# Subtractions of a recurrence moved to TensorE, scaling moved to ScalarE, and a new order of pieces in one stage

## The reference

```
x = x + tanh(g_xattn[0]) * attention_over_heads(layernorm(x), ctx)     # stages A, B, G0
x = x + tanh(g_ffn[0])   * mixture_of_16_experts(layernorm(x))         # top 6 and a shared one: G0, H0
x = x + tanh(g_xattn[1]) * wkv(w, u, k=layernorm(x), v=ctx)            # stage M
x = x + tanh(g_ffn[1])   * mixture_of_64_experts(layernorm(x))         # top 8: routing in M, then H1, I1

def layernorm(x): return (x - mean) / sqrt(var + 1e-5)
def wkv step, per sequence and channel, over 64 positions (p, q, o are carried):
    no  = max(o, u + k);   A  = exp(o - no);      E  = exp(u + k - no)
    y   = (A * p + E * v) / (A * q + E)
    no2 = max(w + o, k);   A2 = exp(w + o - no2); E2 = exp(k - no2)
    p, q, o = A2 * p + E2 * v, A2 * q + E2, no2
```

## Time and profile before

| what | us |
|---|---|
| median of 3 runs (2355.72 to 2356.34) | 2355.81 |
| the profiled execution's own time | 2351.87 |
| its span, first to last instruction | 2350.1 |
| stage M, about | 1229 to 1754 |

### The profile page before, as it was taken

One profiled execution on the slowest core, in us unless ns is written; L12 is line 12 of the kernel. 1 busy time (PEld: TensorE's weight loads), 2 busy tenths in 40 slices (PEclk: granted clock), 3 DMA queues, 4 the chain that ended last, 5 costly groups with the idle time before them and its releaser, 6 DMA issues. The chain is left out here.

```text
span 2350.1 us, 35817 instructions
## 1 busy us (share of the span) xinstructions
PE 1636.8 (70%) x9250; PEld 1208.8 (51%) x9250; DVE 1325.7 (56%) x3592; ACT 682.7 (29%) x1894; POOL 1045.3 (44%) x1039
## 2 busy tenths in 40 slices
PE   2959976888439999999964344441109999999800
PEld 1437754555227777777742222221108888888700
DVE  5113325656315555555536999999705555555557
ACT  1422221222013333333322222222005555555400
POOL 4031003677733333333330166666656666666600
PEclk9979986988769999999987666665559999999955
DMA  4595646533435757666314244544766666666489
GB/s 142 182 147 69 97 63 245 186 120 114 160 112 183 264 195 245 211 229 225 114 60 171 89 158 159 177 148 160 260 260 184 190 187 194 191 190 192 147 336 378
DMA packets 237104, 419.22 MB, mean 178 GB/s; under 512 B 90496, under 2 KB 170496, under 8 KB 231424
## 3 DMA queue, kind: packets, MB, share of 16 engines
q1 hardware_dynamic: 164080, 215.58, 32.3%
q0 software_dynamic: 48144, 138.57, 16.1%
q10 hardware_dynamic: 24704, 62.98, 7.7%
HBM read 253.36 MB, written 209.88 MB: 197 GB/s over the span
## 5 line engine op out<-in xcount | busy, mean ns | idle before, releaser
L896 PE MATMUL ps<-w_all,h_xT 128*128 x2112 | 546.1, 381 | 5.2 <-ACT h_xT L1119 5.2
L913 PE MATMUL ps<-w_all,h_hT 89*128 (+1 forms) x1472 | 409.7, 383 | 2.5
L640 POOL DMA_INDIRECT y_b<-h_y,h_ix x320 | 310.1, 969 | 174.9 <-issue 127.9
L623 POOL DMA_INDIRECT xs_b<-h_x,slot_of x256 | 270.9, 1058 | 244.0 <-DVE slot_of L1474 168.2
L896 PEld LDWEIGHTS ps<-w_all,h_xT 128*128 128x128 f32 x2112 | 343.3, 191 | 53.3 <-issue 9.2
L640 POOL DMA_INDIRECT y_a<-h_y,h_ix x208 | 201.7, 970 | 350.0 <-DVE h_y L1638 341.1
L889 PE MATMUL ps<-ident,h_x 128*128 128x128 f32 x1056 | 203.8, 274 | 115.3 <-DMA h_x<-xs_a 61.2
L1638 DVE TENSOR_SCALAR h_y<-ps,h_sum 128x256 f32<-128x256 f32 x528 | 254.6, 482 | 38.6 <-issue 22.8
L913 PEld LDWEIGHTS ps<-w_all,h_hT 89*128 89x128 f32 (+1 forms) x1472 | 239.2, 191 | 29.8 <-issue 6.5
L1119 ACT COPY h_xT<-ps 128x256 f32<-128x256 f32 x528 | 196.1, 371 | 151.9 <-PE ps L889 136.0
L623 POOL DMA_INDIRECT xs_a<-h_x,slot_of x192 | 190.0, 990 | 105.9 <-issue 57.9
(11 more groups left out here) (232 smaller groups left out, 2129.4 us busy)
## 6 DMA issues: line engine op xcount, KB each, us to landing
xs_b<-void_d ACTq DMA_DIRECT2D x40, 1128.0 KB, 13.1
h_x<-xs_b SPq DMA_DIRECT2D x80, 564.0 KB
c_a<-y_b SPq DMA_DIRECT2D x8, 4096.0 KB, 13.1
h_x<-xs_a SPq DMA_DIRECT2D x52, 564.0 KB, 4.2
k_a<-y_a SPq DMA_DIRECT2D x16, 1536.0 KB, 8.2
w_all<-in_exp SPq DMA_DIRECT2D x7, 2560.0 KB
qkv_d<-a_out ACTq DMA_DIRECT2D x8, 1536.0 KB, 7.4
w_all<-in_exp SPq DMA_DIRECT2D x4, 2432.0 KB
```

What stands on the lines that cost most here:

```text
L623: pool.indirect_dma_start(xs_d[L.name], bass.IndirectOffsetOnAxis(ap=slot_of[:, g * GT + j, k:k + 1], axis=0), h_x[:, g % NB, j, :], None) ...
L640: pool.indirect_dma_start(y_d[L.name], bass.IndirectOffsetOnAxis(ap=h_ix[:, s:s + 1], axis=0), h_y[:, s % YB, :], None).then_inc(q["y_st"] ...
L896: m = pe.matmul(ps[:, 2 + s % 2, 0:2 * L.H], h_xT[:, s % 2, c, :], w_all[:, bass.ds(e * L.W + c * 2 * L.H, 2 * L.H)], start=(c == 0), stop ...
L913: m = pe.matmul(ps[:, 6 + s % 2, 0:D], h_hT[0:w, s % 2, j, :], w_all[0:w, bass.ds(e * L.W + L.up0 + j * D, D)], start=(j == 0), stop=(j == ...
```

## The change

It has three parts. First, the four differences of the recurrence are no longer made by DVE: for each, PE adds two products into one PSUM bank, one of an identity with the first operand and one of a negated identity (`minus`) with the second, and ACT reads the bank with the exponential; three banks (5, 6, 7) take turns, and u is added as the bias of the exponential. DVE keeps the scan and the maximum. Second, both normalisations become a scale and a shift on ACT: DVE only makes 1/std and -mean/std (`scale_of`), ACT runs four passes over 128x256 (`scaled`). Third, the pieces stand in another order on PE, ACT and DVE, and PSUM banks are dealt anew: `choices_summed` moves from banks 2, 3 to 0, 1, which it shares with `states_back`. The diff, cut to its core:

```
-            w_o = s_("w_o", [P, GB, SEQ + 1])
-            w_t = s_("w_t", [P, KC, 4, GB, SEQ])
+            w_o = s_("w_o", [P, KC, GB, SEQ + 1])
+            minus = s_("minus", [P, P])
...
-        turn_bank = {"a": 2, "b": 4}
-        logit_bank = {"a": 2, "b": 6}
-        rank_bank = {"a": 3, "b": 7}
+        turn_bank = {"a": 2, "b": 2}
+        logit_bank = {"a": 2, "b": 4}
+        rank_bank = {"a": 3, "b": 4}
+        spread = (5, 6, 7)
...
+            def differences(g, c):                                             # PE
+                o_prev, o_now = w_o[:, c, :, 0:SEQ], w_o[:, c, :, 1:SEQ + 1]
+                key, largest = w_k[:, c, :, 1:SEQ + 1], w_max[:, c]
+                pe.wait_ge(wk_t, 2 * g + c + 1)
+                for v, (a, b) in enumerate(((o_prev, o_now), (key, o_now), (o_prev, largest), (key, largest))):
+                    n = 4 * (2 * g + c) + v
+                    if n >= 3:
+                        pe.wait_ge(wk_exp, n - 2)
+                    pe.matmul(ps[:, spread[n % 3], :], ident[:], a, start=True, stop=False)
+                    pe.matmul(ps[:, spread[n % 3], :], minus[:], b, start=False, stop=True).then_inc(wk_less, 1)
...
             def choices_summed(g):
-                    if g:
-                        pe.wait_ge(k_used, g)
+                    if g >= 2:
+                        pe.wait_ge(wk_yu, g - 1)
...
+                if g < NG:                                                     # PE, round g
+                    differences(g, 0)
+                    differences(g, 1)
+                if g:
+                    turned(L1, g - 1)
+                    logits(L1, g - 1, e_g1)
                 if g + 1 < NG:
                     choices_summed(g + 1)
                 if g:
-                    turned(L1, g - 1)
-                    logits(L1, g - 1, e_g1)
                     ranks(L1, g - 1)
...
+            def scaled(g, dst):                                                # ACT
+                for j in range(GT):
+                    t = g * GT + j
+                    m = act.activation(dst[:, j, 0:D], x_res[:, t, :], ACT.Identity, bias=mean[:, t:t + 1],
+                                       scale=rstd[:, t:t + 1])
+                return m
...
                 if g < NG:                                                     # ACT, round g
                     decays(g, 0)
+                    decays(g, 1)
                 if g:
                     deviations(L1, g - 1)
-                if g < NG:
-                    decays(g, 1)
-                if g:
+                    rows_normalised(g - 1)
                     turned(L1, g - 1)
                     exponentials_of(L1, g - 1)
                 if g + 1 < NG:
                     key_deviations(g + 1)
+                    keys_normalised(g + 1)
                     keys_turned(g + 1)
...
+            def scale_of(part):                                                # DVE
+                dve.reciprocal(rstd[:, part], rstd[:, part])
+                dve.drain()
+                return dve.scalar_tensor_tensor(mean[:, part], mean[:, part], -1.0, rstd[:, part], ALU.mult, ALU.mult)
...
-                dve.tensor_tensor(w_t[:, c, 0], o_prev, o_now, ALU.subtract)
-                dve.tensor_tensor(w_t[:, c, 1], key, o_now, ALU.subtract)
-                dve.drain()
-                dve.tensor_tensor(w_t[:, c, 2], o_prev, w_max[:], ALU.subtract)
-                dve.scalar_tensor_tensor(w_t[:, c, 3], key, u, w_max[:], ALU.add, ALU.subtract).then_inc(wk_t, 1)
...
                 if g < NG:                                                     # DVE, round g
                     exponents(g, 1)
+                    over_time(g, 0)
                 if g:
-                    normalised_rows(L1, g - 1)
+                    row_scales(g - 1)
                 if g < NG:
-                    over_time(g, 0)
+                    over_time(g, 1)
                 if g:
                     less_largest(L1, g - 1)
                 if g + 1 < NG:
                     choices_added(g + 1)
                 if g:
                     chosen_experts(L1, g - 1)
-                if g < NG:
-                    over_time(g, 1)
+                if g + 1 < NG:
+                    keys(g + 1)
                 if g:
                     slots_of(L1, g - 1)
-                if g + 1 < NG:
-                    keys(g + 1)
                 if g < NG:
                     divided(g)
```

More of the change, by code:

```diff
@@ L224, in flamingo @@
             w_ev = s_("w_ev", [P, GB, SEQ + 1])
-            w_max = s_("w_max", [P, GB, SEQ])
+            w_max = s_("w_max", [P, KC, GB, SEQ])
             w_p = s_("w_p", [P, KC, GB, SEQ + 1])
@@ L1178, in key_deviations, with keys_normalised, rows_normalised @@
                 act.activation(rstd[:, part], mean_v[:, part], ACT.Sqrt).then_inc(wk_std, 1)
+            def scaled(g, dst):
[4 more added lines that the diff above has]
+                return m
+            def keys_normalised(g):
+                act.wait_ge(wk_scale, g + 1)
+                scaled(g, w_n1).then_inc(wk_xn, 1)
+            def rows_normalised(g):
+                act.wait_ge(g_scale, g + 1)
+                scaled(g, h_x[:, g % NB]).then_inc(g_norm, 1)
             def keys_turned(g):
@@ L1182, in keys_turned @@
                 for c in range(KC):
-                    m = act.copy(w_k[:, c, :, 1:SEQ + 1], ps[:, 4 + c, :].rearrange("p (b t) -> p b t", t=SEQ))
+                    m = act.copy(w_k[:, c, :, 1:SEQ + 1], ps[:, 2 + c, :].rearrange("p (b t) -> p b t", t=SEQ))
                 m.then_inc(wk_k, 1)
             def decays(g, c):
-                act.wait_ge(wk_t, 2 * g + c + 1)
-                act.activation(w_a2[:, c, :, 1:SEQ + 1], w_t[:, c, 0], ACT.Exp, bias=w_wu[:, c:c + 1])
-                act.activation(w_e2[:, c, :, 1:SEQ + 1], w_t[:, c, 1], ACT.Exp)
-                act.activation(w_ex[:, c].rearrange("p j b t -> p (j b t)"),
-                               w_t[:, c, 2:4].rearrange("p j b t -> p (j b t)"), ACT.Exp).then_inc(wk_e, 1)
+                outs = (w_a2[:, c, :, 1:SEQ + 1], w_e2[:, c, :, 1:SEQ + 1], w_ex[:, c, 0], w_ex[:, c, 1])
+                shifts = (w_wu[:, c:c + 1], None, None, w_wu[:, KC + c:KC + c + 1])
+                for v in range(4):
+                    n = 4 * (2 * g + c) + v
+                    src = ps[:, spread[n % 3], :].rearrange("p (b t) -> p b t", t=SEQ)
+                    act.wait_ge(wk_less, n + 1)
+                    if shifts[v] is None:
+                        act.activation(outs[v], src, ACT.Exp).then_inc(wk_exp, 1)
+                    else:
+                        act.activation(outs[v], src, ACT.Exp, bias=shifts[v]).then_inc(wk_exp, 1)
             key_deviations(0)
             act.wait_ge(wk_pad, 1)
+            keys_normalised(0)
             keys_turned(0)
@@ L1717, in choices_added, with keys, row_scales @@
                 moments_of(g, wk_var)
-            def keys(g):
-                part = slice(g * GT, g * GT + GT)
-                dve.wait_ge(wk_std, g + 1)
+            def scale_of(part):
                 dve.reciprocal(rstd[:, part], rstd[:, part])
                 dve.drain()
-                for j in range(GT):
-                    t = g * GT + j
-                    m = dve.tensor_scalar(w_n1[:, j, :], x_res[:, t, :], mean[:, t:t + 1], rstd[:, t:t + 1],
-                                          ALU.subtract, ALU.mult)
-                m.then_inc(wk_xn, 1)
+                return dve.scalar_tensor_tensor(mean[:, part], mean[:, part], -1.0, rstd[:, part], ALU.mult, ALU.mult)
+            def keys(g):
+                dve.wait_ge(wk_std, g + 1)
+                scale_of(slice(g * GT, g * GT + GT)).then_inc(wk_scale, 1)
+            def row_scales(g):
+                part = slice(g * GT, g * GT + GT)
+                if g >= NB:
+                    dve.wait_ge(lay["b"]["row_st"][g % NB], 16 * GT * L1.K * (g // NB))
+                dve.tensor_copy(h_x[:, g % NB, :, RW - CH1 - 1:RW], tail[:, part, :])
+                dve.wait_ge(g_std, NG + g + 1)
+                scale_of(part).then_inc(g_scale, 1)
             def flat(ap):
@@ L1733, in exponents @@
             def exponents(g, c):
-                key = w_k[:, c, :, 1:SEQ + 1]
-                o_prev, o_now = w_o[:, :, 0:SEQ], w_o[:, :, 1:SEQ + 1]
-                u = w_wu[:, KC + c:KC + c + 1]
                 dve.drain()
@@ L1740, in exponents @@
                     dve.wait_ge(wk_k, g + 1)
[L1741 removed]
+                if g:
+                    dve.wait_ge(wk_less, 4 * (2 * (g - 1) + c + 1))
+                dve.tensor_tensor_scan(flat(w_o[:, c]), flat(w_dec[:, c]), flat(w_k[:, c]), 0.0, ALU.add, ALU.max)
                 dve.drain()
[L1743 to L1748 removed]
+                dve.scalar_tensor_tensor(w_max[:, c], w_k[:, c, :, 1:SEQ + 1], w_wu[:, KC + c:KC + c + 1],
+                                         w_o[:, c, :, 0:SEQ], ALU.add, ALU.max).then_inc(wk_t, 1)
             def over_time(g, c):
```

21 lines of the change are left out of this document (11 added, 10 removed).

## The result

The changed kernel takes 2427.27 us (median of 4 runs, 2426.73 to 2431.48), the kernel before 2356.07 on the same chip (4 runs): a ratio of 1.0301, 95% interval 1.0284 to 1.0317, slower by 3.0%. The forecast was 2415 (2390 to 2432), and slower with 0.94. The profiled execution took 2427.13 us with a span of 2425.2, which is 75.1 more than before.

The account below looks back on a forecast made before the run. DVE was taken to bound M's rounds; four waits of 16.8 us against 7.9 saved. Start +1.1, round 0 +4.6, six rounds +53.4, round 7 +0.3 sum to +59.4: 2411.3 profiled, 2415 as median, range 2390 to 2432.

Parts of the forecast that it names:

- the wait for the choices behind the logits: Rounds of stage M: DVE's choices_added waits from 29.3 to 39.0 us for PE's 12 products, 9.7 us.
- 2.4, 1.9, 2.6 and 9.7: DVE's forecast waits in a round of M, in us: for exponentials, square root, logits, and the choices' products.
- The mis-sized term: PE's 12 products of the choices behind the logits: 10.5 us, clock back near their start, done at 39.0.
- rival 5: ACT in M's rounds: as much lost again behind each table load, 1.28 x 6, total 2423; chance 0.04.
- Round 0: First round of M: clock up at about 6, choices at 28.2, round 40.9 us, +4.6.
- ACT's four passes: Rows' normalisation on ACT in a round of M: 2.25 us taken, done at 21.6; range 1.4 to 2.9.
- DVE's gain: DVE in a round of M: differences 5.26 and two normalisations 1.3 each saved, together 7.9 us.
- Costs put at nothing: ACT's and PE's keys work under slots and divided, SP's loads and write of x, POOL's last two groups: 0.
- 1 (DVE stays the bound, 2296): Rounds of M: choices ready when DVE reaches choices_added, rounds 46.4 us, sum -59.4, 2296; chance 0.02.
- 2 (no gap on PE, 52.1 to 53): PE in M's rounds: no gaps at all, rounds 52.1 to 53 us, 2342 to 2356; chance 0.03.
- 3 (the clock holds): PE's 5.0 us gap in M's rounds: clock stays up, rounds 60.3 us, 2398; chance 0.10.
- 4 (the clock stays down in the differences): PE's differences in M: half clock because of semaphore pauses, 16 products at 1.72 us, 2588; chance 0.03.

Follow-up runs that it names:

- the filler run of the second set: Changed kernel plus five products nobody reads in PE's gap between differences and transposes: 2409.14 us, ratio 1.0243; in the first set, on a slower chip, 1.0406.
- the last kernel: Kernel with choices cut in two, plus first reciprocal moved into the square-root wait and two first-half differences back on DVE: ratio 0.9836 on a slower chip.
- the last two: Kernel with choices cut in two, first reciprocal moved into the square-root wait: 0.9933; with two first-half differences also back on DVE: 0.9836; slower chip.

## Why the prediction was right, point by point

- **The bound.** That DVE's round is not what its work adds up to, and that the wait for the choices behind the logits is the largest of four, was right. The order alone loses 69 of the 73 us with the same wait, and putting the 12 products first takes the wait away and 7 us off a round. Waits of 2.8, 1.8, 2.4 and 10.8 stand against 2.4, 1.9, 2.6 and 9.7. (These four add up to 16.6; the prediction's 16.8 is the round less 46.4.)
- **The mis-sized term** is the 12 products at 10.5 us, "the clock comes back near their start". They took 11.75 to 12.06, because the clock came back 2.9 us after their start. In round 3 the logits are there after 28.9 us and not 28.5, the choices after 40.6 and not 39.0, and behind them DVE needs 23.9 and not 24.2. So a round is 64.7 in the mean and not 63.2: 9 of the 15.7 us that the sum fell short.
- **How the forecast of the clock was made.** It took from the earlier trace rows that the clock fell 4.0 us after the long products. PE was not idle for these 4.0 us, as this row of the kernel before shows; the clock fell at 1367.1 after short work between pauses of 1.89 and 1.16 us:

```profile
1364.99 1.09 PE L798 MATMUL ps<-ident,h_x 128*128 128x128 f32 x8 [1.89 <-DVE h_x L1360]
```

- **How near the number came.** The 2427 lies at the upper end of the forecast's own range of 2403 to 2428; the terms that it names reach only from 2404 to 2425. And 4.3 of the 15.7 us lie outside stage M. By the time alone rival 5, at 2423, came nearer than the forecast; it is the trace that rules it out.
- **Round 0**: 42.6, not 40.9. There too the clock: it came up 8.4 us after the scan (0.94 over 1272 to 1273), where 6 was taken, so the choices were ready 29.6 us in and not 28.2.
- **ACT's four passes** took 2.08 us and 0.49 of signal from DVE ahead of them, against 2.25 with little for the signal. The prediction had the second operand per partition from a single comparison of rows. The Trainium skill, "ScalarE: Activation LUTs", section "What ACT_TABLE_LOAD costs", states 186 ns + 0.833 ns per column, 93 ns more for each such operand and an overlap of 93 ns. As an estimate by that page the four passes take 4 x 0.585 - 3 x 0.093 = 2.06 us, and the trace agrees with its 2.08.
- **DVE's gain** of 7.9 us of work was right in kind: busy time fell by 7.4. But the prediction set 7.9 saved against 16.8 of waits, and the runs show that most of both is the same time: with the order alone DVE has the logits 28.7 us into the round and with the moves as well 28.9, so the work taken away ahead of them turned into waits.
- **Costs put at nothing** held: the keys' chain under slots and divided, SP's loads (both `k_a` loads now go at 1341, in mid-round), the last two groups of POOL (91.74 against 91.64). One sign missed: POOL idles 21.7 to 22.1 us before groups 1 to 5, and not 18 to 20, since the rounds are 1.5 us longer than forecast and a group costs it about 42.8 us and not 44.3.
- **Rivals.** 1 (DVE stays the bound, 2296) fell: its condition, that the choices are ready when DVE arrives, was made true by cutting them in two, and even then two waits kept the round at 52.9 and not 46.4. 2 (no gap on PE, 52.1 to 53) was not this kernel; its numbers fit that experiment, 52.9 and 2354, in which PE has no gap above 1.2 us from states_back to the second six products. 3 (the clock holds) fell with the 0.64 at 1456; the filler run of the second set shows what it would have given, 2409, where the prediction said 2398. 4 (the clock stays down in the differences) fell with 0.86 a product. 5 (a drain behind the table load) fell: the load ends at 1453.06 + 1.28 = 1454.34 and the square root begins at 1454.35. The Trainium skill, "ScalarE: Activation LUTs", section "What ACT_TABLE_LOAD costs", has 1.38 us of drain for each switch, and this trace does not show it.
- **Outside M**: +2.9 ahead of it and +1.4 behind, in stages that the change does not touch. Run again, the changed kernel began M at 1229.88, 0.6 from before, so most of that is from one execution to the next.

## What to carry to other kernels

Work taken from the busiest engine bought nothing here, since the chain that runs beside it through the others was not shorter than what was left. So add up that chain with its hops before the move, up to each point where the engine waits. Look at what is queued behind such a point on the helper engine: here six needed products moved from behind the logits into a gap, with one piece of DVE's work drawn ahead of their use, made up the whole 3%. And a helper whose clock falls around its pauses pays for the gap twice (4.0 us a round here beside the idle time), so fill its gaps with work that is needed anyway, and the waiting engine's with work that nobody waits for.

## What the runs showed of the hardware that was not expected

- After a pause the granted clock came back 3.4 us after PE's first instruction in round 2 of the kernel before, and in round 3 of the change 4.3 us after the first and 9.5 us after the second restart of the round, the latter across a pause of 1.16 us between transposes and logits. In the kernel with the choices cut in two, successive rounds of the same code differ: 6.6 us in round 3 and 4.1 in round 4 (from 1410.01 to 0.69 of full clock over 1416 to 1417, and from 1463.69 to 0.93 over 1467.69 to 1468.69), which goes with waits for w_ev of 3.93 and 2.37 us. What sets it is open.
- The chips differ by 11% on one kernel (2618.66 and 2617.60 us on two of them, 2354.83 on another), and also in the stages ahead of M, which are the same in all of these kernels: M begins at 1229 to 1233 us on the ordinary chips and at 1329 to 1338 on the slower ones. On the slower ones short instructions stand idle with no releaser in M's later rounds. The mean of the rows' statistics, round 2 of the last kernel:

```profile
1488.65 1.41 DVE L1388 BATCH_NORM_STATS2 stats<-x_res 128x6 f32<-128x256 f32 x4
1491.66 0.17 DVE L1390 TENSOR_TENSOR tmp_t<-stats 128x4 f32<-128x4 f32 x1 [1.60 <-issue]
```

In round 1 the same pair has a gap of 0.07 us (1436.97 + 1.41, then 1438.45). What makes these idle times, no run here tests. From round 1 to the mean of the later rounds the kernels lost 0.4 us (all differences on DVE), 4 to 5 (the last two), 4 to 9 (choices first) and 12 to 14 (scaling on DVE, filler). What tells them apart is open.
